# A plan of its own for the first batch of a fused attention kernel

## The chip, the cores and the metric

The kernel runs on one NeuronCore of a Trainium2 chip, as a single launch. The time is device microseconds of that core, from the start of the launch to its end; lower is better. The engines named below are TensorE (PE: matmuls and transposes), VectorE (DVE), ScalarE (ACT), GpSimd (POOL) and SyncE (SP, which issues most transfers).

## What is computed

The input is x of 8 batches by 1024 tokens by 256 features. The reference does a mixture-of-experts step, causal attention with 16 heads of 16 features, and a second mixture-of-experts step:

```
x = x + 0.5 * ffn(layernorm(x))
x = x + attn(layernorm(x))
x = x + 0.5 * ffn(layernorm(x))

attn:  q = x @ Wq.T + bq;   k, v = split(x @ Wkv.T + bkv)
       dots = (q * scale) @ k.T, masked above the diagonal
       out = (softmax(dots) @ v) @ Wo.T + bo
ffn:   top 2 of 8 experts; an expert chosen more than cap times adds nothing
       (keep = counts <= cap)
```

With these inputs every expert is over its cap, so the kernel computes the gate logits, top 2 and counts for both layers, finds that no expert is kept, and skips the expert work. What takes the time is attention.

## The kernel before

**Steps and units.** Each batch is done in NG = 4 steps, one for each group of four heads. A step has NU = 48 units, and in every unit TensorE does one score matmul `st` (keys by queries, L1306), whose exponential ScalarE takes (L867). Every fourth unit adds a group of `pv` matmuls (L1340) that multiply exponentials into the values. In the same unit TensorE does one more score matmul `s` (queries by keys, L1321) for a later step: VectorE takes its row maximum (L1027 with the causal mask on diagonal blocks, L1031 elsewhere), so that a step knows its maxima before it starts. The 48 maxima of a step are 16 diagonal ones (four each of 128, 256, 384 and 512 columns) and then 16 pairs of a full block (512 columns) and a diagonal one; the mean is 384 columns. `s` has three PSUM banks, so an `s` matmul waits until the maximum three units before it is taken.

**The lead.** Maxima run EARLY = 15 units ahead: unit u of step h does the maximum u + 15, counted from the start of step h + 1. So before the first step of the first batch a prologue must do the 48 maxima of that step and 15 of the next. Number them i = 0 to 62. In the prologue TensorE has little to do, and a `warm` matmul on a constant (L1349) fills each unit that has no other work.

**From maxima to scores.** When half of a step's maxima are there, VectorE splits them into three bf16 parts in four or five small operations (`mfin`, L1042 to L1050), TensorE turns them (`mtr`, L1289), and ScalarE copies them into rows of `q_stack` (L854), where the `st` matmul reads them as extra contraction rows. The first `st` of all waits for the `mtr` of both halves.

**Queries and keys.** For each head group hq and half c (512 tokens) there is a projection `use qk hq c` (L1222, four fp32 matmuls, eight records in the trace). ScalarE evicts it twice (L827), GpSimd subtracts (L751), VectorE casts (`q2`, L1121), GpSimd subtracts again (`q3`, L757), and SP writes the three bf16 parts to `part_dram` (L636). After c = 1 SP loads all nine pieces of `q_stack` and `k_stack` of that group (L654, L659). ScalarE's eviction for (hq, c) first waits until the parts of (hq - 1, c) have been written, since it overwrites them. The prologue does all four groups: (0, 0), (0, 1), (1, 0) ahead of the maxima, and the other five fills at the units in `pro_qk`. For group 0 the loads are split by half: SP issues six pieces of `k_stack` (L645), ScalarE three of `q_stack` (L903, `qload`).

**The order.** It is written out by hand: `step_plan`, `batch_plan` and `prologue_plan` make one list of events, and every engine walks that list and issues what is its own (`handle`). Each engine is in order. `put(u, ...)` places an event behind unit u.

**Output side.** `otr` scales and turns a step's output, `ont` turns it to features by tokens, and ScalarE evicts that into `o_t` with the value bias `v_bias` added, as two activations of 256 columns (L848). `wo` multiplies by Wo (L1206), and `bo` adds `bo_row` on GpSimd (L762).

## Time and profile before

| | |
|---|---|
| time, median of 3 runs | 1365.62 us (1365.21 to 1366.24) |
| the profiled execution: time | 1366.13 us |
| its span in the trace | 1364.3 us |
| busy: PE, DVE, ACT, POOL | 92%, 80%, 69%, 29% of the span |
| mean granted TensorE clock | 0.983 |

The profile is of one execution. Engine time counts an instruction from its start to its end, and pipelined instructions overlap, so the distance between two starts is less than the duration of one. A granted clock of 1.00 is 2.4 GHz, 0.50 is 1.2 GHz. The span leaves out 1.8 us of the profiled time, which lie around the program.

### The profile page before, as it was taken

The numbers are of one execution on the slowest core, as the hardware profiler recorded it, in microseconds if no ns is written. First come the engines' busy times: TensorE is split into PE (matmuls) and PEld (weight loads), VectorE is DVE, ScalarE is ACT, GpSimd is POOL, SyncE is SP. The second block draws the span as 40 slices with busy tenths as digits, with TensorE's granted clock in tenths as the row PEclk, the third lists the DMA queues.
The fourth block names the chain that finished last, engine by engine and source line by source line (L and its number), as shares of the span: only waits on it lengthen the run. The fifth ranks groups of instructions, "written<-read, shape, count | busy, mean of one in ns | idle before, by whom it ended". The sixth has DMA issues, their size and how long they took to land.

```text
span 1364.3 us, 25092 instructions
## 1 busy us (share of the span) xinstructions
PE 1257.0 (92%) x8697; PEld 600.3 (44%) x8697; DVE 1092.6 (80%) x3521; ACT 940.5 (69%) x1697; POOL 397.8 (29%) x508
## 2 busy tenths in 40 slices
PE   7789999999999999999999999999999999999874
PEld 5333344444454444454444444544445544444332
DVE  5798888778887888878887788878888788789744
ACT  2257776777767777767777777677777677776752
POOL 4323332322232322332323333323222323222111
PEclk9989999999999999999999999999999999999887
DMA  5770333542325444334435433254342143330001
GB/s 143 137 126 13 71 70 59 101 91 57 69 39 101 90 70 71 60 65 89 70 59 101 71 75 69 40 101 90 70 71 55 33 96 71 59 71 31 1 1 34
DMA packets 57832, 95.18 MB, mean 70 GB/s; under 512 B 8352, under 2 KB 51488, under 8 KB 51744
## 3 DMA queue, kind: packets, MB, share of 16 engines
q1 hardware_dynamic: 54800, 91.52, 35.8%
q10 hardware_dynamic: 2896, 1.98, 0.6%
q8 instruction: 70, 1.15, 0.4%
q14 instruction: 66, 0.54, 0.1%
HBM read 59.91 MB, written 33.55 MB: 69 GB/s over the span
## 4 chain that ended last, share of the span: by engine, by line
PE 60%; DVE 23%; ACT 7%; issue 4%; DVEq 3%; POOL 2%; DMA 1%; SPq 1%; ACTq 0%; POOLq 0%
PE o_bank L1340 15%; PE s L1321 13%; PE st L1306 12%; DVE s L1027 10%; PE misc L1222 6%; PE misc L1206 4%; PE misc L1214 4%; DVE max_full L1031 3%; ACT probs L867 3%; PE misc L547 3%; DVEq L1040 2%; ACT q_stack L854 2%; DVE xn L523 1%; DMA part_dram<-parts 1%; DVE stats L514 1%
## 5 line engine op out<-in xcount | busy, mean ns | idle before, releaser
L867 ACT ACTIVATE probs<-st 128x512 f32<-128x512 f32 (+1 forms) x1216 | 632.8, 582 | 191.0 <-PE st L1306 120.9
L1027 DVE CUSTOM_DVE_ANT_0 s<-s,causal 128x128 f32<-128x128 f32 (+3 forms) x1024 | 496.4, 506 | 118.2 <-PE s L1321 113.3
L1321 PE MATMUL s<-k_stack,q_stack 96*128 96x512 bf16 (+3 forms) x1536 | 494.9, 332 | 36.3 <-DVE max_diag L1027 17.9
L1306 PE MATMUL st<-q_stack,k_stack 108*128 108x512 bf16 (+3 forms) x1536 | 484.9, 328 | 12.8 <-ACT probs L867 12.2
L1031 DVE TENSOR_REDUCE max_full<-s 128x1 f32<-128x512 f32 x512 | 349.8, 683 | 44.0 <-PE s L1321 44.0
L1340 PE MATMUL o_bank<-probs,v_aug 128*17 128x512 f32 (+3 forms) x3072 | 324.9, 495 | 5.5 <-POOL probs L739 5.3
L1321 PEld LDWEIGHTS s<-k_stack,q_stack 96*128 96x128 bf16 x1536 | 149.5, 98 | 369.5 <-DVE max_diag L1027 161.2
L739 POOL TENSOR_SCALAR_AFFINE_SELECT probs<-probs 128x512 f32<-128x512 f32 x256 | 162.8, 636 | 468.3 <-ACT probs L867 467.9
L1306 PEld LDWEIGHTS st<-q_stack,k_stack 108*128 108x128 bf16 x1536 | 150.5, 98 | 98.3 <-ACT probs L867 37.4
L751 POOL TENSOR_TENSOR qk<-qk,parts 128x512 f32<-128x512 f32 x64 | 74.5, 1164 | 280.5 <-ACT parts L827 280.5
L1027 DVE DVE_READ_ACCUMULATOR2_ANT max_diag<- 128x1 f32 x1024 | 144.0, 141 | 0.1
L854 ACT ACTIVATE q_stack<-misc 12x2048 bf16<-12x2048 f32 x62 | 115.9, 1869 | 29.9 <-PE misc L1289 29.4
L1222 PE MATMUL misc<-x_t,w_qk 128*128 128x256 f32 x464 | 122.0, 385 | 4.1 <-ACT o_t L848 4.1
L757 POOL TENSOR_TENSOR parts<-qk,parts 128x512 bf16<-128x512 f32 x64 | 76.9, 1201 | 119.2 <-DVE parts L1121 119.1
L1340 PEld LDWEIGHTS o_bank<-probs,v_aug 128*17 128x17 f32 x3072 | 51.2, 95 | 125.8 <-issue 99.4
L1222 PEld LDWEIGHTS misc<-x_t,w_qk 128*128 128x128 f32 x464 | 84.6, 190 | 25.5 <-ACT o_t L848 8.0
L827 ACT ACTIVATE qk<-misc,qk_bias,qk_scale 128x512 f32<-128x512 f32 x58 | 45.1, 777 | 71.0 <-PE misc L1222 63.7
L1206 PE MATMUL misc<-w_o,o_t 128*128 128x256 f32 x248 | 64.4, 386 | 5.4 <-ACT parts L827 4.6
L523 DVE TENSOR_SCALAR xn<-x_all,mean_var,rstd 128x256 f32<-128x256 f32 x128 | 59.5, 474 | 8.6 <-POOL rstd L530 6.6
L1214 PE MATMUL misc<-w_v,x_t 128*128 128x256 f32 x232 | 60.8, 385 | 0.0
L1206 PEld LDWEIGHTS misc<-w_o,o_t 128*128 128x128 f32 x248 | 45.4, 190 | 22.9 <-DVE o_tok L1128 6.8
L514 DVE BATCH_NORM_STATS2 stats<-x_all 128x6 f32<-128x256 f32 x128 | 52.6, 420 | 3.3 <-issue 0.4
(113 smaller groups left out, 886.0 us busy)
## 6 DMA issues: line engine op xcount, KB each, us to landing
part_dram<-parts SPq DMA_DIRECT2D x128, 192.0 KB, 2.8
k_stack<-part_dram SPq DMA_DIRECT2D x186, 128.0 KB, 7.3
q_stack<-part_dram SPq DMA_DIRECT2D x31, 384.0 KB, 4.9
x_all<-x SPq DMA_DIRECT2D x16, 512.0 KB, 11.5
q_stack<-part_dram SPq DMA_DIRECT2D x31, 256.0 KB, 7.4
out<-x_all SPq DMA_DIRECT2D x7, 1024.0 KB, 11.2
q_stack<-part_dram SPq DMA_DIRECT2D x31, 128.0 KB, 8.9
k_stack<-part_dram SPq DMA_DIRECT2D x12, 64.0 KB, 4.2
```

Of the source, the lines that this page charges most:

```text
L739: nc.gpsimd.affine_select(out=now, in_=now, compare_op=ALU.is_ge, fill=0.0, base=0, pattern=[[0, HG], [1, P]], channel_multiplier=-1)\
L757: nc.gpsimd.tensor_tensor(parts[:, c, 2, :], qk32[:, :], parts[:, c, 1, :], ALU.subtract)\
L854: nc.scalar.activation(q_stack[rows, hm, :, c * CW:(c + 1) * CW], bank[rows, :].rearrange("p (o c) -> p o c", o=1) .to_broadcast([MROWS, H ...
L867: nc.scalar.activation(probs[:, g % 2, h - part:h + 1, 0:width], st_bank[i % 3][:, 0:share * width] .rearrange("p (h c) -> p h c", c=width ...
L1027: nc.vector.tensor_tensor_reduce(out=bank, in0=bank, in1=causal[:, CW - width:CW], scale=1.0, scalar=-BIG, op0=ALU.add, op1=ALU.max, accum ...
L1031: nc.vector.tensor_reduce(max_full[:, (hg + ahead) % 2, h, ib - CT:ib - CT + 1], bank, AX.X, ALU.max)\
L1206: last = nc.tensor.matmul(bank[:, t * D:(t + 1) * D], heads[:, dc, t * P:(t + 1) * P], w_o[:, dc, :], start=dc == 0, stop=dc == DC - 1)
L1214: last = nc.tensor.matmul(bank[:, t * D:(t + 1) * D], x_t[:, dc, t0:t0 + P], w_v[:, dc, :], start=dc == 0, stop=dc == DC - 1)
L1222: last = nc.tensor.matmul(bank[:, cols], w_qk[:, dc, hq, :], x_t[:, dc, c * CW:(c + 1) * CW][:, cols], start=dc == 0, stop=dc == DC - 1)
L1306: score = nc.tensor.matmul(st_bank[i % 3][:, part * width:(part + 1) * width], k_stack[0:KROWS + MROWS, hg, h, jb * P:(jb + 1) * P], q_sta ...
L1321: nc.tensor.matmul(s_bank[u % 3][:, 0:width], q_stack[0:KROWS, hm, h, ib * P:(ib + 1) * P], k_stack[0:KROWS, hm, h, j0:j0 + width], start= ...
L1340: last = nc.tensor.matmul(o_bank[32 * h:32 * h + VW, off:CW], v_aug[:, jb, of % NG * HG + h, :], probs[:, g % 2, h, 0:CW - off], start=g i ...
```

## The change

- The prologue does FRONT = 53 maxima instead of 63, which is 5 units of lead at the first score. Over the four steps of batch 0 the lead grows to 15 again (`FRONT_RAMP`): 51, 51, 50 and 50 maxima per step instead of 48. `mfin` and `mtr` in batch 0 follow from that ramp and from `FRONT_MTR`. Later batches keep their plan.
- In the prologue (2, 0) moves from unit 20 to 26 and (2, 1) from 29 to 35. The fills of group 3, which were at units 38 and 47, move into step 0 of batch 0, to units 4 and 16.
- The prologue's second `mtr` is 3 units behind the half, not 6.
- Wo times the value bias is computed once (`bias`, two matmuls, one eviction, one addition on GpSimd) and added to `bo_row`; the two evictions into `o_t` with a bias become one plain copy.
- For group 0, ScalarE issues one of the six `k_stack` pieces of each half instead of SP.

```diff
-    "pro_qk": (10, 20, 29, 38, 47),
+    "pro_qk": (10, 26, 35),
...
+FRONT = NU + 5
+FRONT_RAMP = ((0, FRONT), (NU, 2 * NU + 8), (2 * NU, 3 * NU + 11), (3 * NU, 4 * NU + 13), (4 * NU, 5 * NU + EARLY))
+FRONT_QK = (4, 16)
+FRONT_MTR = {(1, 0): 33, (1, 1): 46, (2, 0): NU + 17, (2, 1): NU + 44, (3, 0): 2 * NU + 13, (3, 1): 2 * NU + 42,
+             (4, 0): 3 * NU + 13, (4, 1): 3 * NU + 43}
...
+def maxima_by(t):
+    for (t0, n0), (t1, n1) in zip(FRONT_RAMP, FRONT_RAMP[1:]):
+        if t <= t1:
+            return n0 + (n1 - n0) * (t - t0) // (t1 - t0)
+def front_maxima():
+    units, more = {}, {}
+    for t in range(NG * NU):
+        for i in range(maxima_by(t), maxima_by(t + 1)):
+            group, u = divmod(i, NU)
+            units.setdefault(t, []).append((group - t // NU, u))
+            for c in range(2):
+                for k in range(MFIN_PARTS[c]):
+                    of, first = divmod(i - HALF_UNITS[c] - k, NU)
+                    if first == 0 and i - k > NU + 1:
+                        more.setdefault(t, []).append(("of", of - 1, "mfin", c, k))
+    for (group, c), t in FRONT_MTR.items():
+        more.setdefault(t, []).append(("of", group - 1, "use", "mtr", c))
+    return units, more
...
+    if hg == 0 and not prev:
+        for c, u in enumerate(FRONT_QK):
+            put(u, ("use", "qk", 3, c))
+            put(u + Q2_LAG, ("q2", 3, c))
+            put(u + Q3_LAG, ("q3", 3, c))
...
+    if not prev:
+        for u in range(NU):
+            put(u, *front_more.get(NU * hg + u, ()))
...
+            if not prev:
+                plan += [("s",) + unit for unit in front_units.get(NU * hg + HG * g + h, ())]
...
+    if spec:
+        plan += [(3, "use", "bias")]
+    plan += [(3, "use", "qk", 1, 0), (3, "qload", 1), (3, "warm", WARM[1])]
...
-    for u in range(NU + EARLY):
+    for u in range(FRONT):
         for c in range(2):
             if u == HALF_UNITS[c]:
                 plan += [(3, "mfin", c, k) for k in range(MFIN_PARTS[c])]
-            if u == HALF_UNITS[c] + 6:
+            if u == HALF_UNITS[c] + (6, 3)[c]:
...
-                        for r, times, part in RUNS:
+                        for r, times, part in RUNS[:2]:
...
+                elif kind == "use" and a[0] == "bias":
+                    eng.wait_ge(sig.misc_free, n("use", 2))
+                    nc.gpsimd.tensor_tensor(bo_row[:, 0, :], bo_row[:, 0, :], xg_t[:, 0, 0:D], ALU.add)
...
+                elif what == "bias":
+                    nc.scalar.activation(xg_t[:, 0, 0:D], bank[:, 0:D], ACT.Copy).then_inc(sig.misc_free, 1)
...
-                    for dc in range(DC):
-                        last = nc.scalar.activation(o_t[:, dc, :], bank[:, dc * 2 * P:(dc + 1) * 2 * P],
-                                                    ACT.Identity, bias=v_bias[:, dc:dc + 1])
-                    last.then_inc(sig.misc_free, 1)
+                    nc.scalar.activation(o_t[:, :, :], pair_view(bank), ACT.Copy).then_inc(sig.misc_free, 1)
...
+                    eng.dma_start(k_stack[rows, 0, :, cols],
+                                  part_dram[0, 1, part, :, cols].rearrange("(d h) c -> d h c", h=HG))\
+                       .then_inc(landed, 16)
...
+                elif what == "bias":
+                    for dc in range(DC):
+                        last = nc.tensor.matmul(bank[:, 0:D], v_bias[:, dc:dc + 1].to_broadcast([P, P]), w_o[:, dc, :],
+                                                start=dc == 0, stop=dc == DC - 1)
```

TensorE at the end of the prologue, before (`st<-ident,max_parts` is the second `mtr`, `o_bank<-causal,ident` a `warm`):

```order
L1321 MATMUL s<-k_stack,q_stack 128x256
L1349 MATMUL o_bank<-causal,ident 128x384
L1321 MATMUL s<-k_stack,q_stack 128x256
L1349 MATMUL o_bank<-causal,ident 128x384
L1289 MATMUL st<-ident,max_parts 128x128 x4
L1321 MATMUL s<-k_stack,q_stack 128x256
L1349 MATMUL o_bank<-causal,ident 128x384
L1321 MATMUL s<-k_stack,q_stack 128x256
```

The same place after the change:

```order
L1373 MATMUL s<-k_stack,q_stack 128x128
L1401 MATMUL o_bank<-causal,ident 128x384
L1341 MATMUL misc<-ident,max_parts 128x128 x4
L1373 MATMUL s<-k_stack,q_stack 128x128
L1401 MATMUL o_bank<-causal,ident 128x384
L1373 MATMUL s<-k_stack,q_stack 128x256
L1401 MATMUL o_bank<-causal,ident 128x384
L1358 MATMUL st<-q_stack,k_stack 128x512
```

The `mtr` stood behind the sixth maximum of the next step, and nine more followed before the first `st`. It now stands behind the third, and two follow.

TensorE a few units into step 0 of batch 0, before:

```order
L1321 MATMUL s<-k_stack,q_stack 128x128
L1306 MATMUL st<-q_stack,k_stack 128x512
L1321 MATMUL s<-k_stack,q_stack 128x512
L1306 MATMUL st<-q_stack,k_stack 128x384
L1321 MATMUL s<-k_stack,q_stack 128x128
```

And after (`misc<-x_t,w_qk` is the projection (3, 0)):

```order
L1373 MATMUL s<-k_stack,q_stack 128x256
L1358 MATMUL st<-q_stack,k_stack 128x512
L1373 MATMUL s<-k_stack,q_stack 128x384
L1358 MATMUL st<-q_stack,k_stack 128x384
L1270 MATMUL misc<-x_t,w_qk 128x256 x2
L1373 MATMUL s<-k_stack,q_stack 128x384
L1270 MATMUL misc<-x_t,w_qk 128x256 x2
L1358 MATMUL st<-q_stack,k_stack 128x384
```

The maxima there are now earlier ones in the row, and the projection stands between them in two pieces.

ScalarE just ahead of the maxima in the prologue, before (`lg_t` is the eviction of the first gate logits):

```order
L827 ACTIVATE qk<-st,qk_bias,qk_scale 128x512
L827 ACTIVATE parts<-st,qk_bias,qk_scale 128x512
L903 DMA q_stack<-part_dram 48x4x512
L903 DMA q_stack<-part_dram 32x4x512
L903 DMA q_stack<-part_dram 16x4x512
L839 ACTIVATE lg_t<-st 128x128
```

And after:

```order
L888 ACTIVATE xg_t<-st 128x256
L876 ACTIVATE qk<-st,qk_bias,qk_scale 128x512
L876 ACTIVATE parts<-st,qk_bias,qk_scale 128x512
L948 DMA q_stack<-part_dram 48x4x512
L948 DMA q_stack<-part_dram 32x4x512
L948 DMA q_stack<-part_dram 16x4x512
L951 DMA k_stack<-part_dram 16x4x512
L890 ACTIVATE lg_t<-misc 128x128
```

The eviction of `bias` comes in ahead of the projection's, and a fourth issue behind the three.

## Rows read from the trace of the kernel before

**Rows 1.** Busy time by engine: us, PE, PEld, DVE, ACT, POOL, PEclk, DMA

```profile
76.48:92.81 16.33, 14.01 (x78) 3.74 (x76) 15.47 (x53) 8.61 (x16) 3.79 (x6) 0.90 0.93 160
127.56:163.66 36.10, 34.32 (x251) 14.42 (x250) 30.16 (x99) 28.78 (x50) 12.15 (x14) 1.00 0.38 67
```

**Rows 2.** The chain that ended last, 50 to 66 us: start, us, what

```profile
52.37 0.42 SPq L659
...
52.84 0.59 SPq L636
53.47 8.72 DMA part_dram<-parts
...
62.26 0.78 ACT qk L827
...
63.85 1.16 POOL qk L751
65.03 0.43 DVE parts L1121
```

**Rows 3.** VectorE in order of time, end of the prologue: start, us

```profile
57.60 0.69 DVE L1031 TENSOR_REDUCE max_full<-s 128x1 f32<-128x512 f32 x1
...
65.38 0.69 DVE L1027 CUSTOM_DVE_ANT_0 s<-s,causal 128x512 f32<-128x512 f32 x1
...
67.43 0.17 DVE L1042 TENSOR_TENSOR max_diag<-max_diag,max_full 128x16 f32<-128x16 f32 x1
...
68.50 1.13 DVE L1050 TENSOR_TENSOR max_parts<-max_rest,max_parts 128x16 bf16<-128x16 f32 x1
```

**Rows 4.** TensorE in order of time, prologue and first score

```profile
27.75 1.89 PE L1222 MATMUL st<-x_t,w_qk 128*128 128x256 f32 x8
29.48 3.41 PE L1349 MATMUL o_bank<-causal,ident 128*128 128x384 bf16 x20
...
58.77 0.60 PE L1222 MATMUL misc<-x_t,w_qk 128*128 128x256 f32 x2
66.27 0.27 PE L1321 MATMUL s<-k_stack,q_stack 96*128 96x128 bf16 x1 [6.90 <-DVE max_diag L1027]
...
71.41 0.63 PE L1289 MATMUL st<-ident,max_parts 128*128 128x128 bf16 x4
...
76.48 0.38 PE L1306 MATMUL st<-q_stack,k_stack 108*128 108x512 bf16 x1
```

**Rows 5.** ScalarE and its queue in order of time, prologue

```profile
32.59 2.14 ACTq L903 DMA_DIRECT2D q_stack<-part_dram  x3
...
72.08 1.87 ACT L854 ACTIVATE q_stack<-st 12x2048 bf16<-12x2048 f32 x1 [3.82 <-PE st L1289]
```

**Rows 6.** Transfers issued from 52.3 to 52.7 us: median us to landing

```profile
k_stack<-part_dram SPq DMA_DIRECT2D x1, 128.0 KB, 9.3
```

**Rows 7.** Busy time by engine, columns as in the first group

```profile
59.00:66.00 7.00, 0.37 (x2) 0.00 (x0) 0.97 (x4) 1.45 (x2) 1.61 (x2) 0.68 0.78 187
70.00:75.00 5.00, 5.00 (x21) 2.86 (x22) 4.38 (x20) 1.87 (x1) 1.15 (x1) 0.50 0.96 129
82.00:85.40 3.40, 3.40 (x16) 1.14 (x16) 3.31 (x12) 0.60 (x1) 0.63 (x1) 0.50 0.95 133
```

**Rows 8.** Who waited for whom, 127.56 to 163.66 us: total, times, longest

```profile
DVE s L1027 <- PE s L1321: 4.0, 5, 1.6
```

**Rows 9.** Who waited for whom, TensorE, whole span

```profile
PE misc L1289 <- DVE max_parts L1050: 5.2, 7, 1.2
```

**Rows 10.** The tile o_t: durations, and who waited for it

```profile
L848 ACT ACTIVATE o_t<-misc,v_bias x62: 466/473/497, 261.1 to 1339.2; 128x256 f32<-128x256 f32 x62
...
PE misc L1222: 4.1, 6
```

**Rows 11.** Costs of groups, 76 to 128 us: busy us, mean ns

```profile
L833 ACT ACTIVATE x_t<-misc 128x512 f32<-128x512 f32 x4 | 2.4, 608 | 0.1
```

**Rows 12.** ScalarE in order of time, one turn of the output in batch 1

```profile
278.91 0.85 ACT L848 ACTIVATE o_t<-misc,v_bias 128x256 f32<-128x256 f32 x2
```

More of the change, by code:

```diff
@@ L146 @@
 WARM = (26, 20, 1)
+FRONT = NU + 5
[21 more added lines that the diff above has]
+    return units, more
 def step_plan(hg, prev, nxt, spec):
+    front_units, front_more = front_maxima() if not prev else (None, {})
     extra, early = {}, {}
@@ L278, in prologue_plan @@
     plan += ones(1) + project(0, 1) + ones(2, 3) + [(3, "use", "v", j) for j in range(2)] + [(3, "qload", 0)]
-    plan += [(3, "use", "v", j) for j in range(2, 4)] + [(3, "use", "qk", 1, 0), (3, "qload", 1), (3, "warm", WARM[1])]
+    plan += [(3, "use", "v", j) for j in range(2, 4)]
+    if spec:
+        plan += [(3, "use", "bias")]
+    plan += [(3, "use", "qk", 1, 0), (3, "qload", 1), (3, "warm", WARM[1])]
     jobs = {4: [(3, "q2", 1, 0)], 6: [(3, "q3", 1, 0)]}
@@ L890, in handle @@
                     eng.wait_ge(sig.late_full, 1)
-                    for dc in range(DC):
-                        last = nc.scalar.activation(o_t_late[:, dc, :], late_bank[0][:, dc * 2 * P:(dc + 1) * 2 * P],
-                                                    ACT.Identity, bias=v_bias[:, dc:dc + 1])
-                    last.then_inc(sig.late_free, 1)
+                    nc.scalar.activation(o_t_late, pair_view(late_bank[0]), ACT.Copy).then_inc(sig.late_free, 1)
                 elif kind == "weights":
```

6 lines of the change are left out of this document (3 added, 3 removed).

## Prediction

> **What bounds the kernel now.** I read busy time by stretch first. In a step of batch 0, TensorE is busy 34.32 of 36.10 us and VectorE 30.16 [rows 1], and VectorE's largest idle there is 4.0 us of waiting for `s` matmuls [rows 8]. So inside a batch TensorE sets the pace, and VectorE has some room. The stretch from the first `st` to the first output eviction (76.48 to 92.81 us, units 0 to 20 of step 0) reads otherwise: VectorE is busy 15.47 of 16.33 us, TensorE 14.01 [rows 1]. There the maxima set the pace.
>
> The view that matters for this change is the chain, in the prologue. Behind the loads of group 1, the last of which is issued at 52.37, SP issues the parts of (2, 0) at 52.84. They land 8.72 us later. ScalarE's eviction of (3, 0) at 62.26 was held until then, GpSimd's subtraction follows at 63.85 and VectorE's cast at 65.03 [rows 2]. That cast stands in VectorE's order ahead of the last three maxima of the step. VectorE's last maximum before it is at 57.60, the next at 65.38 [rows 3]. TensorE, whose `s` banks are then full, does its last work at 58.77 and goes on at 66.27 after 6.90 us of idle [rows 4]. A 7 us hole in both engines thus comes from a projection that no maximum of that moment needs. Behind it TensorE runs at a granted clock of 0.50 (1.2 GHz) to 75 us [rows 7]. The second `mtr` is at 71.41, and the first `st`, which stands behind nine more maxima, at 76.48 [rows 4].
>
> **The change, part by part.** I move along the axis of the trace before.
>
> *Start of the maxima.* `bias` puts two fp32 matmuls ahead of the projection (1, 0). Four such take 1.73 us from start to start (27.75 to 29.48), so two take 0.87, and the 20 `warm` and the first maximum behind them are later by that [rows 4]. ScalarE gets a fourth issue behind three of 2.14 us [rows 5], 0.7 us more before it evicts the first gate logits, for which TensorE waits at the fifth maximum. The two delays lie beside each other. I take 0.7 us, between 0 (if the maxima wait for landings anyway) and 0.87. GpSimd's addition to `bo_row` lies in its idle time and costs nothing; uncovered it would be under a subtraction's 1.2 us (start to start 63.85 to 65.03, [rows 2]). Taking one issue from SP saves SP time, but nothing there waits for SP alone, so I count nothing.
>
> *The hole goes.* With the casts of group 3 gone from the prologue, VectorE goes on at 57.60 + 0.69 = 58.3. The three maxima left take 67.43 - 65.38 = 2.05 us, and the five pieces of `mfin` 68.50 - 67.43 = 1.07 and some 0.2 for the last one alone [rows 3]. The end of `mfin` is 58.3 + 2.05 + 1.3 + 0.7 = 62.3. The moved fills of group 2 keep four casts ahead of that point, as before.
>
> *What is late next.* The 49th maximum is the first of step 1, and it needs group 1 loaded. The last piece, issued at 52.37, takes 9.3 us [rows 6]: 61.7, with the delay 62.4. Before, the hole hid this. TensorE now waits there some 2.3 us (59.4 + 0.7 to 62.4), and the second `mtr` stands behind it. So landing and `mfin` end within 0.1 us of each other. Then come three short maxima with three `warm`, 0.9 us (between 0.65 at the full clock and 1.3 at half), the `mtr` and its way to ScalarE, 72.08 - 71.41 = 0.67, and the eviction of 1.87 us [rows 4, 5]. First `st` at 62.4 + 0.9 + 0.67 + 1.87 = 65.8, against 76.48. **Term one: -10.6 us** (from -9.0 if the landings come 1.6 us later, to -11.5 without the 0.7 us delay).
>
> *Units 0 to 20 of step 0.* The projections (3, 0) and (3, 1) are both in this stretch: 2 x 1.73 = 3.5 us on TensorE, against 16.33 - 14.01 = 2.3 us that it idles there [rows 1, 4]. VectorE gets one more maximum (22 against 21), the ones it does are the 16 diagonal ones and then six instead of others, and one more cast, 0.4 us [rows 2]; about +0.9 us. GpSimd is busy 3.79 of 16.33 us [rows 1], and three subtractions of 1.2 us fit. If only VectorE paces, the stretch costs +0.9; if TensorE's work is added whole, +3.5, and +4.5 if the two ScalarE evictions also hold exponentials. **Term two: +2.5 us**, nearer to TensorE's, as two engines now have no slack.
>
> *The rest of batch 0.* Nine more maxima. On TensorE the mean unit has 384 columns, like a `warm`, and 20 of those take 3.41 us: 0.17 each [rows 4]. On VectorE a unit is at most about 0.68 (2.05 / 3, [rows 3]). TensorE paces and VectorE waits 4.0 us a step [rows 8], so I take 0.25: 2.2 us, from 1.5 to 6.1. One `mtr` is tight: that of (1, 1) is at unit 46 of step 0, one unit behind the last `mfin` piece (before there were three). TensorE's waits at `mtr` are 5.2 us in seven, 1.2 at most [rows 9]; I take 0.3. **Term three: +2.5 us** (1.5 to 7.3).
>
> *The plain copy into o_t.* Two activations take 0.85 us [rows 12]; a copy of the same 512 columns takes 0.61 [rows 11]. That is 0.24 us for each of 31 evictions (62 activations, [rows 10]). TensorE idles behind them 4.1 us in six places, 0.68 each [rows 10], and gets 0.24 back in each: 1.5 us. The other 25 shorten ScalarE's queue, which is mostly hidden; I add 0.5. **Term four: -2.0 us** (-0.5 to -7.5, if all 31 were on the path).
>
> Sum: -10.6 + 2.5 + 2.5 - 2.0 = -7.6 us. Against the profiled execution's 1366.13 that is 1358.5. The median of the runs lies 0.5 under that execution, so **1358.0 us**.
>
> *The clock.* After the 7 us hole the granted clock was 0.68 and then 0.50, and in 82.0 to 85.4, behind a stretch with many small stalls, it was 0.50 again, with TensorE busy all 3.40 us [rows 7]. That second stretch loses 1.7 us. After the change TensorE is nearly idle from 60 to 66 us, so I keep one such stretch at the start of step 0, as before; this cancels in the sum. The Trainium skill (TensorE: Matmul & The Clock Gate, Part 1: The HAM clock gate) says that the throttled state is the default and that activity releases it. By that rule the shorter hole does not save the clock, and the sum stays as it is; the rows agree for a hole of 7 us and say nothing of one of 2.3.
>
> **The rivals.**
> - *The clock holds.* The wait is 2.3 us instead of 6.90, and `warm` matmuls stand on both sides of it. Then the first stretch of step 0 runs at 1.00, the 1.7 us come back and the three maxima ahead of `mtr` take 0.65: 1358.0 - 2.0 = 1356.0 us. For it: the hole is a third as long. Against: behind it comes the eviction of 1.87 us, in which TensorE has two maxima.
> - *The moved work is paid in full.* In units 0 to 20 ScalarE evicts two projections between exponentials, GpSimd subtracts between the selects that `pv` waits for, and VectorE has no slack. Term two becomes +4.5 and term three +4.5: 1362.0 us.
> - *The change does not do what it says.* The loads of group 1 land late. The nine are issued just before the parts of group 2 and share the queues with them. If the last lands at 67 or later, a second hole stands where the first stood, term one is -6 or less, and with the rest on its upper side nothing is left: 1365 us. Against: 9.3 us is a measured landing with the same neighbours.
> - *Slower: the ring of three score banks.* With 5 units of lead instead of 15 in hand, TensorE finds no finished maxima in reserve, and each of the ten added units costs a full turn of a bank, the `s` matmul and the maximum behind it, 0.38 us (as an `st` of 512 columns) + 0.69 us and a handover each way, some 1.3 us [rows 3, 4]. Ten cost 13 us instead of the 2.2 in term three. From 1.0 us a unit on the kernel is no faster; at 1.3 it is 1358.0 + 10.8 = 1368.8 us. Against: VectorE waits for TensorE inside the steps and not the other way round [rows 8].
>
> **How the numbers follow.** Forecast 0.52 (its own range 1356 to 1360.5), clock 0.19, paid in full 0.17, no effect 0.08, slower 0.04. About 0.2% (2.7 us) is what a measurement can tell from no change: faster is below 1362.9, slower above 1368.4. Forecast and clock lie wholly below, and most of the third: faster 0.86. The rest of the third and the fourth give same 0.10, the last slower 0.04. The range must reach over the clock and most of the third, with terms three and four on their better sides below: 1353.5 to 1363.0 us.
>
> **What would show it.** The first `st` at 65 to 67 us. No idle over 4 us on TensorE in the prologue, and the 49th maximum the one it waits for, until about 62.4, by a landing. VectorE without idle from 36 us to `mfin`. Units 0 to 20 longer than 16.33 us by 1 to 4.5, with (3, 0) and (3, 1) in it. Each later step of batch 0 longer by 0.3 to 1.5 us. The steps of later batches shorter by some 0.3 us in the one with `ont`, no more. The prediction is wrong if group 1 lands late, if the first stretch of step 0 stalls on exponentials or selects, or if the copy into `o_t` gives far more than 0.24 us in six places.

## The result and the profile after

| | us, median | runs |
|---|---|---|
| before, run beside it | 1365.41 | 6 |
| after | 1372.25 (1371.37 to 1376.35) | 6 |

The ratio is 1.0052, interval 1.0040 to 1.0064: the change makes the kernel slower by half a per cent, where 1358.0 us was forecast. The profiled execution took 1372.48 us, its span is 1370.7 us (before 1364.3): 6.4 us more to be found.

In every step one ScalarE eviction of the output bank comes at unit 20, so the distance from there to the same eviction of the next step is a step's length whatever the code. It runs from unit 20 of one step to unit 20 of the next. The busy time by engine between these points, after the change (columns as in [rows 1]); the first row is from the first `st` to the first eviction:

```profile
67.62:92.61 24.99, 20.23 (x94) 9.66 (x95) 16.05 (x55) 11.02 (x20) 7.19 (x9) 0.77 0.42 67
92.61:135.44 42.83, 35.75 (x238) 14.45 (x236) 34.64 (x112) 29.23 (x50) 12.22 (x15) 0.96 0.42 81
135.44:172.41 36.97, 34.83 (x248) 14.29 (x247) 31.00 (x99) 26.98 (x50) 12.22 (x14) 1.00 0.37 65
172.41:208.05 35.64, 33.64 (x244) 14.14 (x243) 30.28 (x99) 26.72 (x48) 9.62 (x12) 1.00 0.39 68
208.05:246.10 38.05, 37.41 (x247) 18.12 (x246) 32.79 (x108) 26.56 (x51) 9.79 (x13) 1.00 0.32 52
```

The missing row of the kernel before, for the second of these, and between its first and second eviction:

```profile
92.81:127.56 34.75, 32.22 (x230) 13.38 (x228) 30.79 (x106) 27.23 (x50) 11.04 (x14) 1.00 0.08 21
```

Set side by side (steps of batch 0, in us):

| | first `st` at | units 0 to 20 | four steps from there | their sum |
|---|---|---|---|---|
| before | 76.48 | 16.33 | 34.75, 36.10, 35.18, 37.01 | 143.04 |
| after | 67.62 | 24.99 | 42.83, 36.97, 35.64, 38.05 | 153.49 |
| difference | -8.86 | +8.66 | +8.08, +0.87, +0.46, +1.04 | +10.45 |

The prologue gave 8.9 us, and the first batch took back 19.1. Behind the last of these steps another 3.8 us were gained, which makes the 6.4. VectorE, which had 4 us to spare in a step, is busy 34.64 us in the long one. The mean granted clock of the program is 0.978 (before 0.983).

The prologue went by the prediction's script. TensorE in order of time (the last maximum ahead of the wait, the second `mtr`, the first `st`):

```profile
63.72 0.29 PE L1373 MATMUL s<-k_stack,q_stack 96*128 96x128 bf16 x1 [2.39 <-DMA k_stack<-part_dram]
...
64.98 0.63 PE L1341 MATMUL misc<-ident,max_parts 128*128 128x128 bf16 x4
...
67.62 0.59 PE L1358 MATMUL st<-q_stack,k_stack 108*128 108x512 bf16 x1 [1.05 <-issue]
```

At the end of the prologue there is one wait over 2 us, at the 49th maximum and by a landing, and it ends 1.3 us later than the 62.4 forecast. The `st` takes 0.59 us, where one at the full clock takes 0.38 [rows 4]: TensorE is at 1.2 GHz there.

The chain that ended last through the long stretch, by line, before and after:

```profile
by line: PE o_bank L1340 19.2%; PE s L1321 16.4%; PE st L1306 15.0%; ACT probs L867 11.2%; ACT q_stack L854 7.3%; PE misc L1222 5.7%; issue 5.1%; PE misc L547 3.8%; POOL probs L739 3.6%; POOL x_all L762 3.5%; POOL qk L751 3.3%; ACT qk L827 
```

```profile
by line: PE st L1358 12.3%; PE o_bank L1392 11.4%; PE s L1373 11.1%; ACT probs L915 10.2%; issue 9.8%; DVE s L1075 7.1%; DVE max_full L1079 6.0%; PE misc L1270 4.5%; DVE max_rest L1094 3.2%; ACT q_stack L902 3.2%; DVEq L1088 3.1%; DVE stats
```

Before, no line of VectorE is among the first of it. After, its maxima and `mfin` (`DVE s`, `max_full`, `max_rest`) are. The waits of TensorE in that stretch, all but some short ones and one of 0.77 us for an exponential at 121.62:

```profile
112.76 0.38 PE L1341 MATMUL misc<-ident,max_parts 128*128 128x128 bf16 x4 [1.16 <-DVE max_parts L1098]
...
115.73 0.39 PE L1358 MATMUL st<-q_stack,k_stack 108*128 108x512 bf16 x1 [1.26 <-ACT probs L915]
...
126.86 0.23 PE L1373 MATMUL s<-k_stack,q_stack 96*128 96x128 bf16 x1 [0.82 <-DVE max_full L1079]
...
127.51 0.39 PE L1373 MATMUL s<-k_stack,q_stack 96*128 96x512 bf16 x1 [0.36 <-DVE max_diag L1075]
...
128.39 0.23 PE L1373 MATMUL s<-k_stack,q_stack 96*128 96x128 bf16 x1 [0.43 <-DVE max_full L1079]
129.31 0.39 PE L1373 MATMUL s<-k_stack,q_stack 96*128 96x512 bf16 x1 [0.70 <-DVE max_diag L1075]
```

They come in two places: at 112.76 at the `mtr` of (1, 1) and at the `st` behind it, and in a row from 126.86, all on maxima. I also counted `st` by `st` how far the changed kernel falls behind the one before, from unit 20 on, with the units numbered on from step 0. At unit 46 it is 0.4 us behind, at unit 49 (the first place) 2.8, at unit 61 still 2.9, at unit 65 (the second place) 6.0, and at the end 8.1. The last 2 us come behind unit 65, which is unit 17 of step 1. There the changed kernel has the `mtr` of (2, 0), which was at unit 39 before. VectorE at the second place, after its first wait nearly each operation right behind the one before:

```profile
123.25 0.69 DVE L1079 TENSOR_REDUCE max_full<-s 128x1 f32<-128x512 f32 x1 [1.07 <-PE s L1373]
124.03 0.36 DVE L1092 CAST max_parts<-max_diag 128x16 bf16<-128x16 f32 x1
124.26 0.31 DVE L1075 CUSTOM_DVE_ANT_0 s<-s,causal 128x128 f32<-128x128 f32 x1
124.50 0.13 DVE L1075 DVE_READ_ACCUMULATOR2_ANT max_diag<- 128x1 f32 x1
124.50 0.41 DVE L1169 CAST parts<-qk 128x512 bf16<-128x512 f32 x1
125.01 1.19 DVE L1094 TENSOR_TENSOR max_rest<-max_diag,max_parts 128x16 f32<-128x16 f32 x1
126.12 0.68 DVE L1079 TENSOR_REDUCE max_full<-s 128x1 f32<-128x512 f32 x1
126.89 0.21 DVE L1096 CAST max_parts<-max_rest 128x16 bf16<-128x16 f32 x1
126.98 0.32 DVE L1075 CUSTOM_DVE_ANT_0 s<-s,causal 128x128 f32<-128x128 f32 x1
127.37 0.08 DVE L1075 DVE_READ_ACCUMULATOR2_ANT max_diag<- 128x1 f32 x1
127.54 0.23 DVE L1098 TENSOR_TENSOR max_parts<-max_rest,max_parts 128x16 bf16<-128x16 f32 x1
127.64 0.69 DVE L1079 TENSOR_REDUCE max_full<-s 128x1 f32<-128x512 f32 x1
128.25 0.25 DVE L1174 RECIPROCAL sum_inv<-misc 128x16 f32<-128x16 f32 x1
128.57 0.42 DVE L1176 TENSOR_TENSOR o_tok<-misc,sum_inv 128x256 f32<-128x256 f32 x1
```

Between five maxima stand four operations of `mfin` (L1092 to L1098), the cast of a projection (L1169), and the two of `otr` (L1174, L1176). Before, the same kinds of work lay apart:

```profile
115.29 0.59 DVE L1046 TENSOR_TENSOR max_rest<-max_diag,max_parts 128x16 f32<-128x16 f32 x1
...
116.57 0.21 DVE L1048 CAST max_parts<-max_rest 128x16 bf16<-128x16 f32 x1
...
117.27 0.23 DVE L1050 TENSOR_TENSOR max_parts<-max_rest,max_parts 128x16 bf16<-128x16 f32 x1 [0.24 <-issue]
...
121.42 0.56 DVE L1121 CAST parts<-qk 128x512 bf16<-128x512 f32 x1
...
123.29 0.26 DVE L1126 RECIPROCAL sum_inv<-misc 128x16 f32<-128x16 f32 x1
123.62 0.42 DVE L1128 TENSOR_TENSOR o_tok<-misc,sum_inv 128x256 f32<-128x256 f32 x1
```

`mfin` was over at 117.5, the cast came at 121.4, `otr` at 123.3.

### The profile page after: what moved, and what is told of

The parts are those of the page before. It is cut to its first block, busy times and chain, and to the rows that moved or that the text cites. A ratio compares the mean times of both kernels' runs of the same rounds, so it can differ in the third digit from the quotient of the medians.

```text
span 1370.7 us, 25064 instructions
## 1 busy us (share of the span) xinstructions
PE 1266.1 (92%) x8699; PEld 605.0 (44%) x8699; DVE 1092.7 (80%) x3521; ACT 933.8 (68%) x1666; POOL 399.3 (29%) x509
## 3 DMA queue, kind: packets, MB, share of 16 engines
q8 instruction: 70, 1.15, 0.4%
## 4 chain that ended last, share of the span: by engine, by line
PE 61%; DVE 23%; ACT 6%; issue 4%; DVEq 3%; POOL 1%; DMA 1%; SPq 0%; POOLq 0%; ACTq 0%
PE o_bank L1392 15%; PE s L1373 13%; PE st L1358 12%; DVE s L1075 9%; PE misc L1270 6%; PE misc L1254 4%; PE misc L1262 4%; DVE max_full L1079 3%; ACT probs L915 3%; PE misc L593 3%; DVEq L1088 2%; ACT q_stack L902 2%; DVE xn L569 2%; DVE stats L560 1%; DVE o_tok L1176 1%
## 5 line engine op out<-in xcount | busy, mean ns | idle before, releaser
L1079 DVE TENSOR_REDUCE max_full<-s 128x1 f32<-128x512 f32 x512 | 349.9, 683 | 53.1 <-PE s L1373 52.7
```

The lines of the kernel that those rows point to most:

```text
L1079: nc.vector.tensor_reduce(max_full[:, (hg + ahead) % 2, h, ib - CT:ib - CT + 1], bank, AX.X, ALU.max)\
```

## The experiments

The theory after the result (A): the ramp costs the time, since a short lead leaves TensorE and VectorE waiting for each other; moving the fills and the bias part are each worth something. Its rivals: the moved fills cost it (B), the clock does (C), the place of an `mtr` does (M). Each kernel was timed against the one before on the same chip. Its stretches are read as in the table above.

| kernel | us | ratio, interval | first `st` | units 0 to 20 | four steps |
|---|---|---|---|---|---|
| e1_bias | 1363.80 | 0.9984 [0.9975, 0.9993] | 76.43 | 16.33 | 34.74, 36.12, 35.18, 37.01 |
| e2_move | 1362.25 | 0.9972 [0.9963, 0.9981] | 67.75 | 20.99 | 34.76, 36.12, 35.19, 37.01 |
| e3_ramp | 1378.56 | 1.0085 [1.0071, 1.0099] | 75.98 | 18.83 | 46.69, 37.44, 35.64, 38.05 |
| e4_warm | 1371.64 | 1.0041 [1.0028, 1.0055] | 66.19 | 22.54 | 43.27, 36.96, 35.64, 38.04 |
| e5_both | 1362.36 | 0.9966 [0.9955, 0.9978] | 71.64 | 19.53 | 34.75, 36.12, 35.18, 37.00 |
| e6_mtr | 1371.81 | 1.0040 [1.0027, 1.0053] | 68.53 | 25.13 | 42.33, 37.43, 35.66, 38.05 |
| e7_flat | 1364.28 | 0.9982 [0.9973, 0.9991] | 70.13 | 21.22 | 38.00, 35.95, 34.74, 37.13 |
| e8_late | 1375.74 | 1.0063 [1.0050, 1.0076] | 66.58 | 23.17 | 38.49, 41.96, 38.55, 38.68 |
| e9_mid | 1364.34 | 0.9986 [0.9977, 0.9995] | 65.89 | 22.30 | 38.37, 35.43, 34.90, 37.90 |
| e10_fast | 1367.57 | 1.0007 [0.9998, 1.0016] | 68.00 | 26.42 | 39.94, 35.93, 34.75, 37.12 |
| e11_flatmtr | 1362.12 | 0.9970 [0.9958, 0.9982] | 69.42 | 21.11 | 34.75, 36.11, 35.18, 37.01 |
| e12_best | 1359.67 | 0.9947 [0.9933, 0.9960] | 69.72 | 21.20 | 34.75, 36.12, 35.18, 37.00 |
| e13_mid_mtr | 1363.59 | 0.9977 [0.9966, 0.9987] | 68.66 | 22.31 | 36.40, 35.65, 35.04, 37.67 |
| e14_mid_best | 1362.05 | 0.9963 [0.9949, 0.9977] | 66.16 | 22.31 | 36.39, 35.64, 35.02, 37.68 |
| e15_fast_mtr | 1366.20 | 0.9992 [0.9983, 1.0001] | 67.62 | 24.75 | 36.87, 36.12, 34.75, 37.01 |

### One part at a time

**e1_bias** is the kernel before with the bias computed once and the plain copy:

```diff
+    if spec:
+        plan += [(3, "use", "bias")]
...
-                        last = nc.scalar.activation(o_t[:, dc, :], bank[:, dc * 2 * P:(dc + 1) * 2 * P],
-                                                    ACT.Identity, bias=v_bias[:, dc:dc + 1])
+                    nc.scalar.activation(o_t[:, :, :], pair_view(bank), ACT.Copy).then_inc(sig.misc_free, 1)
```

> The kernel before with the value bias folded into bo_row and the plain copy into o_t, and nothing else of the change. All theories: the batches after the first took 3.9 us less in the changed kernel's trace than in that of before (2.5 in the six middle ones, 1.35 in the last), and the prologue's start is 0.7 to 1.2 us later. So 1362 to 1363 us, ratio 0.997 to 0.9985, with 0.25 us less in each middle batch. If instead the folding itself costs something that shows in the first batch, it is not faster.

**e2_move** is the kernel before with only the fills moved; it keeps 63 maxima and its lead of 15:

```diff
-    "pro_qk": (10, 20, 29, 38, 47),
+    "pro_qk": (10, 26, 35),
...
+    if hg == 0 and not prev:
+        for c, u in enumerate((4, 16)):
+            put(u, ("use", "qk", 3, c))
```

> The kernel before with only the fills moved: (2,0) and (2,1) to units 26 and 35 of the prologue, (3,0) and (3,1) into step 0 of batch 0, at units 4 and 16. The prologue keeps its 63 maxima and the lead of 15. Theory A (the ramp costs the time: ten more maxima in batch 0 with late mtr's): the 7 us hole goes, the first st comes at 66 to 68 us instead of 76.5, the moved projections cost 3.5 to 5 us, and the kernel is faster, 1360 to 1362 us. Theory B (the moved projections cost the time, in TensorE's work at the half clock and in ScalarE's evictions between exponentials): units 0 to 20 of step 0 take 23 us or more instead of 16.3 and the kernel is no faster than before, 1365 to 1369 us. Theory C (the granted clock): like B, with the half clock covering (3,1) again.

**e3_ramp** is the changed kernel with all five fills back in the prologue, at (10, 19, 27, 35, 43):

```diff
-    "pro_qk": (10, 26, 35),
+    "pro_qk": (10, 19, 27, 35, 43),
...
-FRONT_QK = (4, 16)
```

> The changed kernel with the fills of group 3 back in the prologue (five fills at units 10, 19, 27, 35, 43, since one may not follow another by less than 8 units) and nothing moved into step 0. The hole in front of the cast of (3,0) should be back, 7 us. The first st comes at 70 to 73 us. Theory A (ramp): the rest of batch 0 is still 6 to 8 us longer than before from the first output eviction on, so the kernel is near or above the changed one, 1370 us or more. Theory B (moved projections): units 0 to 20 take 17 us, and the kernel is at 1362 to 1366 us.

**e4_warm** is the changed kernel with 14 `warm` ahead of the 49th maximum and 8 more ahead of the first `st`.

> The changed kernel with 14 more warm matmuls ahead of the 49th maximum (TensorE waits 2.4 us there) and 8 more ahead of the first st (it waits 1 us there at the half clock). They lie in waits. Theory C (the half clock costs the time): the clock stays at 1.00 from 61 to 72 us, (3,0) is done in 1.7 us less, and the kernel is 3 to 5 us faster than the changed one, 1367 to 1369 us. Theories A and B: 2 us at most, the same stalls come later, 1370 to 1372 us.

Measured, and this settles theory A, with the places of the `mtr` still in it, against B and C. The bias part gives 2.5 us and the moved fills 4.1 (against 1366.31 us for the kernel before in this series); e3_ramp, which has the ramp and the bias part but no fill in step 0, is 12 us slower. Its first `st` came at 76 us and not at 70 to 73, and some of the 12 us is clock: in its step of 46.69 us the granted clock was 0.89, in the changed kernel's 0.96. The steps of e2_move are those of the kernel before to 0.02 us: the fills in step 0 cost time in their own stretch and nowhere else. Busy time of the stretch from the first `st` in e2_move, e3_ramp and e4_warm, and of the next one in the last two:

```profile
67.75:88.74 20.99, 16.90 (x94) 7.41 (x93) 17.36 (x54) 10.82 (x20) 7.20 (x9) 0.92 0.37 63
```

```profile
75.98:94.81 18.83, 15.80 (x78) 5.32 (x79) 15.47 (x54) 8.85 (x16) 3.79 (x6) 0.70 0.90 149
94.81:141.50 46.69, 38.88 (x238) 15.83 (x236) 34.45 (x111) 29.56 (x50) 11.04 (x14) 0.89 0.08 24
```

```profile
66.19:88.73 22.54, 17.82 (x94) 8.31 (x95) 15.72 (x55) 10.60 (x20) 7.19 (x9) 0.85 0.50 82
88.73:132.00 43.27, 35.67 (x238) 14.45 (x236) 34.64 (x112) 29.24 (x50) 12.21 (x15) 0.96 0.44 80
```

In e2_move the fills raise the stretch from 16.33 to 20.99 us. In e4_warm the first `st` came at the full clock and 1.4 us sooner, and the stretch lasted 22.54 instead of 24.99 us. That is 3.9 us at the front, 0.55 of it an earlier start of the maxima (33.37 against 33.92), the rest the clock. But step 0 to 1 stayed at 43.3 us. At the end of the four steps e4_warm was still 3.5 us ahead; 2.5 of these were lost in the later batches, where kernels differ for a reason that stays open (the last section), and by its median it is within 1 us of the changed kernel. So the clock costs something at the front, but C is not the cause of the loss: from the first `st` to the end of the four steps e4_warm took 176.5 us, the kernel before 159.4.

### Does the gain add up?

**e5_both** is e1_bias and e2_move in one.

> Theory A (the ramp costs the time, the moved fills and the bias part save it, and the savings add up): the kernel before with both savings and with its 63 maxima and lead of 15 comes to the time of before less 4.1 us (the moved fills alone) less 2.5 us (the bias part alone): 1359.7 us, ratio 0.995. First st at 68 us, the first output eviction at 89, then steps of 34.8, 36.1, 35.2 and 37.0 us. Theory B (the parts get in each other's way: the bias part delays the start of the maxima by 0.7 us, so the two savings overlap): 1361 to 1362 us, ratio 0.997.

Measured 1362.36 us: the savings do not add up in full (theory B of that text). The first maximum began at 34.3 us in its profile (before 32.7, e2_move 32.2), the landing of group 1 let the 49th go at 64.0 instead of 61.3, and eleven maxima that started at the lower clock stood before the first `st`. In turn its first stretch held the full clock (0.92 in e2_move) and was shorter:

```profile
71.64:91.17 19.53, 15.44 (x94) 6.70 (x93) 17.27 (x54) 10.80 (x20) 7.18 (x9) 1.00 0.35 59
```

### Lead, number of maxima, place of the mtr

Five kernels on these, all with the changed kernel's code. Only e6_mtr and e8_late move an `mtr`; the others keep all of the changed kernel's places:

```diff
 e6_mtr   -FRONT_MTR = {(1, 0): 33, (1, 1): 46, ...
          +FRONT_MTR = {(1, 0): 33, (1, 1): NU + 5, ...
 e7_flat  -FRONT = NU + 5
          +FRONT = NU + EARLY
          +FRONT_RAMP = ((0, FRONT), (4 * NU, 5 * NU + EARLY))
 e8_late  +FRONT_RAMP = ((0, FRONT), (2 * NU, 3 * NU + 5), (4 * NU, 5 * NU + EARLY))
 e9_mid   +FRONT = NU + 10
 e10_fast +FRONT_RAMP = ((0, FRONT), (NU, 2 * NU + EARLY), (4 * NU, 5 * NU + EARLY))
```

> The changed kernel with one mtr moved: that of (1, 1) from unit 46 of step 0, one unit behind the last piece of mfin, to unit 5 of step 1. TensorE's two waits there were 1.16 us at the mtr and 1.26 us at the st behind it. If they are paid as such, step 0 to 1 falls from 42.8 to 40.4 us and the whole to 1369.8 us, ratio to the kernel before 1.003. Theory A (VectorE has more to do per step than it can, and TensorE meets that wherever it looks): the waits only move to the next s, and the time stays at 1372 us, ratio 1.005, within 0.5 us.

> The changed kernel with a flat ramp: 63 maxima in the prologue, 48 in every step, a lead of 15 throughout; the two mtr of each step stay at the places of the changed kernel, and so do the fills and the bias part. Theory A (short lead and the ten added maxima cost the time): as the kernel before with both savings, 1360 us, ratio 0.996, steps of batch 0 34.8, 36.1, 35.2 and 37.0 us. Theory B (the places of the mtr and the pieces of mfin in batch 0 cost it): step 0 to 1 stays above 40 us and the time above 1366 us.

> The changed kernel with the ramp laid otherwise: the prologue still does 53 maxima, the lead stays 5 through steps 0 and 1 (48 maxima each) and grows to 15 in steps 2 and 3 (53 each), with the mtr put 5 units behind the half where the lead is 5. Theory A1 (the number of maxima per step costs, about 2.5 us for each three): step 0 to 1 falls below 40 us and steps 2 and 3 grow by 2 to 3 us over those of the changed kernel. Theory A2 (the short lead costs, because the wide maxima and the small operations of mfin and q2 fall together with other units of st, whatever their number): step 0 to 1 stays at 42 to 43 us and the next one, 37.0 us in the changed kernel, rises to 40 or more; the whole 1374 us or above, ratio 1.006 or more.

> The changed kernel with half the ramp: 58 maxima in the prologue, a lead of 10 at the first score that grows to 15 over the four steps (50, 49, 49 and 49 maxima); mtr, fills and bias part as in the changed kernel. With 63 and a flat lead that kernel took 1364.3 us, with 53 it takes 1372. Theory L (each maximum added to the batch costs the same): half way, 1368 us, ratio 1.0013. Theory T (a threshold: 15 units of lead have slack that 10 units still have and 5 don't): 1365 to 1366 us, ratio 0.9995, step 0 to 1 about 38.5 us. If it is above 1370 us, nearly all of the loss comes with the first five units of lead.

> The changed kernel with all ten added maxima in step 0 (58 there, 48 in the three steps after; lead 15 from unit 48 on). Theory A2 (the short lead costs, the added maxima cost some 0.25 us each): the stretch from the first st to the end of step 1 gets longer than in the changed kernel by seven maxima, 1.8 us, less what the longer lead gives back; steps 2 and 3 (35.6 and 38.1 us in the changed kernel) fall to 34.8 and 37.1; the whole 1370 to 1372 us, ratio 1.003. Theory A1 (VectorE can't do more than 50 maxima in a step): step 0 pays 1 us and more for each of the seven, and the whole is 1376 us or above, ratio 1.007.

**e6_mtr**: step 0 to 1 fell by 0.50 and the next rose by 0.46 us; nothing came back, and the time is that of the changed kernel. **e8_late** has two steps of 48 maxima, none added, at a lead of 5:

```profile
89.75:128.24 38.49, 33.48 (x235) 13.39 (x233) 31.76 (x108) 29.33 (x51) 12.28 (x15) 1.00 0.47 90
128.24:170.20 41.96, 36.78 (x249) 15.12 (x247) 31.20 (x101) 27.74 (x50) 12.15 (x14) 0.96 0.33 58
```

They took 38.49 and 41.96 us instead of 34.75 and 36.10 (the second with 4% less clock), so 3.7 and 5.9 us a step with no maximum added. The late `mtr` at unit 5 is in both, and in the first also that of (2, 0) at unit 17 of step 1, so not all of it is the lead alone. Each theory has half of it: the first fell below 40 us (A1), the second rose over 40 (A2), and the whole is over A2's 1374 us. **e10_fast** has the same ten added maxima as the changed kernel, all in step 0:

```profile
94.42:134.36 39.94, 35.03 (x241) 13.72 (x239) 34.55 (x117) 29.41 (x51) 12.21 (x15) 1.00 0.46 86
```

From the first `st` to the end of the four steps it took 174.16 us, the changed kernel 178.48: more maxima sooner is cheaper, since the lead is back sooner. A1 had asked for 1376 us or more, 1367.6 were measured, below even A2's 1370, and steps 2 and 3 came back to 34.8 and 37.1 us as A2 had it. So the steps at a short lead are the cost, and not the number of maxima. **e9_mid**, with 58 maxima, is as fast as e7_flat with 63, so the loss is not proportional to the maxima (theory T): nearly all of the 8 us between 63 and 53 of them come with the last five units of lead.

**e7_flat** surprised, for neither of its theories holds: with a lead of 15 throughout, step 0 to 1 took 38.00 us, not 34.75 and not over 40. Three kernels went after that. They have the `mtr` of (1, 1) earlier, **e11_flatmtr** at 40 (from e7_flat), **e13_mid_mtr** at 42 (from e9_mid) and **e15_fast_mtr** at 41 (from e10_fast). All three also move the `mtr` of (2, 0) from unit 17 of step 1 to unit 39, out of the stretch from step 0 to 1, and those of (3, 1) and (4, 1) by one to three units. In e11_flatmtr:

```diff
-FRONT_MTR = {(1, 0): 33, (1, 1): 46, (2, 0): NU + 17, (2, 1): NU + 44, ...
+FRONT_MTR = {(1, 0): 33, (1, 1): 40, (2, 0): NU + 39, (2, 1): NU + 44, ...
```

> The kernel with the flat ramp (63 maxima, lead 15), and in addition the mtr of batch 0 at the units that they had before the change ((1, 1) at unit 40 of step 0 instead of 46, (2, 0) at 39 instead of 17). With the changed kernel's places, steps 0 to 1 to 4 took 38.0, 35.95, 34.7 and 37.1 us; before, 34.8, 36.1, 35.2 and 37.0. If the late mtr of (1, 1) costs that 3.2 us, step 0 to 1 falls to 34.8 and the whole to 1361.5 us, ratio 0.9965. If something else in the changed code does (the order of events inside a unit), step 0 to 1 stays at 38 us and the time at 1364 us.

> The kernel with 58 maxima in the prologue (lead 10 growing to 15), with mtr (1, 1) at unit 42 of step 0 instead of 46 and the others at or beside their places before the change. With 46 its steps 0 to 1 to 4 took 38.4, 35.4, 34.9 and 37.9 us. Theory M (the late mtr is a term of its own, 2.2 us over the batch as with the flat lead): step 0 to 1 35.5 us, the whole 1362.1 us, ratio 0.9968. Theory L (at a lead of 10 the wait would move to the next s as it did with a lead of 5): step 0 to 1 stays at 38 us, the whole 1364 us, ratio 0.9985.

> The kernel with 53 maxima in the prologue and all ten added ones in step 0, with mtr (1, 1) at unit 41 of step 0 instead of 46 and the others at or beside their places before the change. With 46 its steps took 39.9, 35.9, 34.8 and 37.1 us. Theory M (the late mtr is a term of its own): step 0 to 1 falls by 3 us to 37, the whole by 2.2 us to 1365.4, ratio 0.9991. Theory L (the mtr's place doesn't matter while the maxima are late): step 0 to 1 stays at 39.5 to 40 us, the whole 1367.6 us, ratio 1.0007.

The step in e7_flat and e11_flatmtr, and in e15_fast_mtr, which stands against the row of e10_fast:

```profile
91.35:129.35 38.00, 32.84 (x235) 13.73 (x233) 31.38 (x108) 29.17 (x51) 12.21 (x15) 1.00 0.47 91
```

```profile
90.53:125.28 34.75, 32.15 (x230) 13.36 (x228) 30.89 (x106) 27.23 (x50) 12.20 (x15) 1.00 0.51 99
```

```profile
92.37:129.24 36.87, 34.17 (x236) 13.14 (x234) 33.78 (x115) 27.59 (x50) 12.20 (x15) 1.00 0.50 94
```

The places of the `mtr` cost that step 3.25 us at a lead of 15 (38.00 to 34.75), 1.97 at 10 and 3.07 in the fast ramp; over the four steps 2.8, 1.8 and 3.0 us. Counted `st` by `st`, each pair runs alike from unit 20 to the first moved `mtr`. Up to unit 65, ahead of the `mtr` of (2, 0), the later place of (1, 1) costs 1.5, 0.3 and 1.35 us. The remaining 1.7 us of each pair come behind unit 65, where (2, 0) stands in the one kernel and not in the other. So the two places share the cost, and at a lead of 10 nearly all of it is that of (2, 0). TensorE and ScalarE in e7_flat, at (1, 1), whose eviction runs from 110.76 for 1.87 us, and at (2, 0):

```profile
110.84 0.38 PE L1358 MATMUL st<-q_stack,k_stack 108*128 108x512 bf16 x1
...
113.31 0.39 PE L1358 MATMUL st<-q_stack,k_stack 108*128 108x512 bf16 x1 [1.21 <-ACT probs L915]
```

```profile
126.01 1.87 ACT L902 ACTIVATE q_stack<-misc 12x2048 bf16<-12x2048 f32 x1
...
128.55 0.39 PE L1358 MATMUL st<-q_stack,k_stack 108*128 108x512 bf16 x1 [1.11 <-ACT probs L915]
```

The `st` at 110.84 is the first of step 1. It belongs to the first half of the tokens, does not need this eviction, and starts while it runs. What waits is a later `st`, for a score bank: for 1.87 us ScalarE takes no exponential. Both places cost in this way.

By the ratios of the runs the places are worth 1.6, 1.2 and 2.0 us, less than in the profiles, and the intervals of each pair overlap. e11_flatmtr and e15_fast_mtr came as theory M had it; e13_mid_mtr (36.40 us, 1363.59 us) lies between its two theories. e15_fast_mtr also bounds what a maximum costs: its step holds six added ones and is 2.1 us over 34.75, 0.35 each. The changed kernel's ramp forces the place of (1, 1), since the last piece of `mfin` comes only at unit 45; the fast ramp, with the same 53 maxima at the start, has it at unit 39. The place of (2, 0) is not forced in either: the last piece of its `mfin` is at unit 11 of step 1 in the slow ramp and at unit 4 in the fast one. No run has the changed kernel's slow ramp with (2, 0) at 39.

e11_flatmtr (1362.12 us) is the changed kernel without its ramp and its places, and it is as fast as e5_both (1362.36 us). So the two parts that no experiment took alone, the issues moved to ScalarE and the prologue's earlier `mtr`, show no effect.

### The better version

**e12_best** is e5_both with `bias` at unit 45 of the prologue, **e14_mid_best** is e13_mid_mtr with the same:

```diff
-    if spec:
-        plan += [(3, "use", "bias")]
...
     if spec:
+        jobs.setdefault(45, []).append((3, "use", "bias"))
```

> The kernel before with the moved fills, the plain copy and the bias part, but with bias at unit 45 of the prologue instead of ahead of the maxima. With it ahead, the maxima began later, the granted clock was 0.50 from 64 to 69 us and the first st was at 71.6 instead of 67.75 us without it. If the place of bias is what costs those 2.4 us to the first output eviction, the savings of 4.1 and 2.5 us now add up: 1359.7 us, ratio 0.995, first st by 68 us. If the clock falls at that place whatever stands ahead, 1362 us, ratio 0.9965, as with bias ahead.

> The kernel of e13_mid_mtr (58 maxima in the prologue, mtr (1, 1) at unit 42) with bias at unit 45 of the prologue instead of ahead of the maxima. Beside the kernel with 63 maxima and the same late bias (1359.7 us) it has five maxima less ahead of the first st (2 to 2.5 us earlier) and five more in the batch (0.25 us each, 1.3 us). If a lead of 10 costs nothing else: 1358.5 us, ratio 0.994. If the shorter lead costs more than the maxima it saves: 1360 us or above, ratio 0.9955 or more.

e12_best is the fastest of all, 6.8 us under the kernel before in its series (1366.50). The number came as expected, the reason did not. TensorE at the end of its prologue:

```profile
62.85 0.23 PE L1331 MATMUL s<-k_stack,q_stack 96*128 96x128 bf16 x1 [0.56 <-DMA k_stack<-part_dram]
...
64.99 0.23 PE L1331 MATMUL s<-k_stack,q_stack 96*128 96x128 bf16 x1 [1.25 <-DVE max_diag L1033]
...
65.80 0.38 PE L1299 MATMUL misc<-ident,max_parts 128*128 128x128 bf16 x4
...
69.72 0.38 PE L1316 MATMUL st<-q_stack,k_stack 108*128 108x512 bf16 x1
```

The clock is full, the wait for the landing is down to 0.56 us, and a wait of 1.25 us for a maximum follows; the first `st` is at 69.7, not 68, and the first eviction at 90.92, hardly before e5_both's 91.17. Its profiled execution is 3.0 us shorter (spans 1358.8 and 1361.8): 0.25 us to the first eviction, 0.96 in one step of batch 1 (37.61 against 38.57 us), 1.8 in the last batch. So the place of `bias` is not shown to be the cause, and the intervals of the two overlap. e14_mid_best was to be at 1358.5 us if a lead of 10 cost nothing else; it was 1362.05 us. In its profile the first `st` is 3.6 us sooner than in e12_best, and 1.1 us come back in the first stretch and 1.7 in the steps; that leaves 0.8 at the end of batch 0, which the later batches lose again for a reason that stays open (the last section). A lead of 10 is not shown to be a gain.

## Why the prediction was wrong

**Term one, right.** The hole went away, the 49th maximum waited for a landing, and the second `mtr` and the eviction followed. -8.9 us against -10.6, a little outside the term's own bounds (-9.0 to -11.5). The rest is size: the maxima began 1.2 us later than before (33.92 against 32.73) instead of 0.7, the landing was 1.3 us late, and the three short maxima and the `mtr` ran at the lower clock. And e2_move with 63 maxima and no `bias` has its first `st` at 67.75 us, hardly later. From the first maximum to the first `st` the changed kernel took 33.7 us and e2_move 35.5: ten maxima less saved 1.8 us, at the lower clock, and the later start took nearly all of it. The starts of the first maximum spread from 32.2 to 34.6 us over the profiles, so of this 1.2 us not all belongs to `bias`. Two small slips change nothing here: the parts of (2, 0) landed 8.72 us behind the start of their transfer at 53.47, not behind their issue, and without the 0.7 us delay the term is -11.3, not -11.5.

**Term two, mis-sized.** +8.7 us against +2.5. The moved fills alone are +4.7 (e2_move), just over my upper bound of 4.5, at about the granted clock of before (0.92 and 0.90). The lower clock is at least 2.5 (24.99 in the changed kernel at 0.77, 22.54 in e4_warm at 0.85). The 1.5 us between e4_warm and e2_move (20.99) are the lead and the rest of the clock, which no run takes apart. I had let the clock cancel. It did not, for the stretch began at 1.2 GHz, which the longer prologue before had left behind by then. That a shorter hole would not save the clock came out, but no row decided it, and the runs give no simple rule of the wait's length. After waits of 1.22 us (e2_move) and 2.25 us (e9_mid) at the 49th maximum the matmuls behind stayed at 2.4 GHz. After 2.39 us in the changed kernel they were at 1.2 GHz up to 72.4, well into step 0. After 3.12 us in e7_flat they were so only from 63.8 to 67.2, and the first `st` at 70.13 was at the full clock again.

**Term three, the step that failed.** It priced nine added maxima at 0.25 us each, and an `mtr` at 0.3: +2.5 us. Measured is +10.5. The maxima themselves are cheap as forecast where the lead is long again: the three later steps grew by 2.37 us together for six of them, 0.4 each, and e15_fast_mtr gave 0.35. What the term left out is what a lead of 5 instead of 15, with the `mtr` places that came with it, does to a step with no maximum added: 3.7 and 5.9 us in e8_late. Of the 8.1 us of step 0 to 1, the places of two `mtr` are about 3, by what e15_fast_mtr got back from them. I had 0.3 for one and nothing for (2, 0): I took TensorE's wait at earlier `mtr`s [rows 9] and not the 1.87 us [rows 5] in which ScalarE takes no exponential. The other 5 us are the short lead with three added maxima, and in part the clock, which fell to 1.2 GHz again behind the waits from 126.86 on. Moving the `mtr` of (1, 1) past the step's end does not help at a lead of 5 (e6_mtr), so how much of the 3 us the changed kernel could have had back by itself stays open.

**Why a short lead costs** is read from the trace and was not tested by itself. By that reading the lead decides which units of `st` and which other work the wide pairs of maxima and `mfin` fall together with. At 15, `mfin`, the cast and `otr` came one behind the other; at 5 they came within 5 us, between maxima, and each wait of TensorE for a bank delays the `st` behind it.

**Term four, right.** -2.0 forecast, -2.5 in e1_bias by the medians, -1.7 between the profiles, nearly all of it as 0.24 to 0.32 us in one step of each of the six middle batches. Of the changed kernel's 3.8 us behind the four steps, only some 1.6 are thus the copy's; 0.96 is one step of batch 1 and the rest the last batch (the last section). The copy takes as forecast, and TensorE's wait for `o_t` fell from 4.1 us [rows 10] to 2.7:

```profile
L898 ACT ACTIVATE o_t<-misc x31: 597/597/619, 271.3 to 1345.5; 128x512 f32<-128x512 f32 x31
```

```profile
PE misc L1270 <- ACT o_t L898: 2.7, 6, 0.4
```

**The rivals.** That of the three score banks had the right sign and near the right time (1368.8 against 1372.25), with the wrong law: a price of 1.3 us for each added maximum. e10_fast, with the same ten in step 0, would then be as slow as the changed kernel, and is 4.7 us faster (by the ratios to the kernel before, 6). My argument against it, that VectorE waits for TensorE inside a step and not the other way round [rows 8], read a property of the lead of 15 as one of the engines. "Paid in full" (+4.5 and +4.5) was right for term two's fills and far too low for term three; "the clock holds" is e4_warm, and its 2 us were real (3.3 at the front), but there only with added `warm`.

## What to carry to other kernels

A lead between a producer and its consumer is more than a reserve: it fixes what coincides with what. Price a shorter one by a step at that lead, not by the number of items that it moves. Idle time that a profile shows with the long lead (4.0 us on VectorE) says nothing about the short one. A long eviction on an engine that others wait for costs by where it stands: here, at a lead of 15, the same 1.87 us were nearly free at units 39 and 40 and cost some 1.5 us each at 46 and 17. And take a bundle apart: two of its parts gave 6.8 us together (e12_best), and the third, the ramp with its `mtr` places, made 0.9966 (e5_both) into 1.0052, 12 us.
